# The beginning reordered: tokens first, quantiser in PSUM, key tiles ahead of the router, GpSimd in pieces of 512

## The reference

```python
x = x + matmul(fake_quant(layernorm(x)), fake_quant(ctx))         # per batch
x = x + moe(layernorm(x))     # 16 experts, 4 groups, top 2 groups, top 2 experts, 1 shared expert
x = x + cross_attention(layernorm(x), ctx)   # 32 heads, 8 KV heads, rms norm of q and k
x = x + lora_experts(x)       # 64 experts of rank 8, top 16

def fake_quant(x, scale, zp):
    return (clip(round(x / scale + zp), 0, 255) - zp) * scale
```

## Time and profile before

| | us |
|---|---|
| median of 3 runs (lowest, highest) | 688.44 (688.21, 688.82) |
| the profiled execution's own time | 687.87 |
| its span, first to last instruction | 686.1 |
| PE, DVE, ACT, POOL busy | 630.3, 435.5, 346.1, 326.9 |
| mean granted TensorE clock | 0.970 |

### The profile page before, as it was taken

One profiled execution on the slowest core, in us unless ns is written; L12 is line 12 of the kernel. 1 busy time (PEld: TensorE's weight loads), 2 busy tenths in 40 slices (PEclk: granted clock), 3 DMA queues, 4 the chain that ended last, 5 costly groups with the idle time before them and its releaser, 6 DMA issues.

```text
span 686.1 us, 11191 instructions
## 1 busy us (share of the span) xinstructions
PE 630.3 (92%) x3004; PEld 281.0 (41%) x3004; DVE 435.5 (63%) x991; ACT 346.1 (50%) x754; POOL 326.9 (48%) x310
## 2 busy tenths in 40 slices
PE   5729989889999999999998599999999979999997
PEld 2314534334444444444443134444444424444453
DVE  5999887354334443855555899999999950000673
ACT  4514535333334333476676677777777743143132
POOL 4923134255445552177878444444444433458111
PEclk9958999899999999999999999999999999999999
DMA  8802035444453433158794999999999995315001
GB/s 330 361 0 76 10 77 93 102 125 138 147 141 123 131 99 123 62 124 218 163 215 92 222 175 188 174 181 182 185 182 182 182 185 158 120 65 183 1 1 62
DMA packets 200314, 95.65 MB, mean 139 GB/s; under 512 B 187962, under 2 KB 188090, under 8 KB 197341
## 3 DMA queue, kind: packets, MB, share of 16 engines
q1 hardware_dynamic: 197490, 90.49, 55.3%
q10 hardware_dynamic: 2795, 4.79, 2.4%
HBM read 48.03 MB, written 1.09 MB: 72 GB/s over the span
## 4 chain that ended last, share of the span: by engine, by line
PE 60%; DVE 18%; issue 8%; POOL 7%; SPq 3%; ACT 2%; DMA 1%; DVEq 0%; POOLq 0%; ACTq 0%
PE ps L276 20%; PE ps L277 19%; PE ps L278 19%; POOL wsp L1042 4%; POOL hlr L1042 3%; SPq L367 3%; DVE st L1165 1%; DVE nw L1177 1%; DVE nw L1176 1%; DVE f32r L1181 1%; DMA stage<-in_first_chunks 1%; DVE xT L1240 1%; PE ps L615 1%; DVE v_sb L1217 1%; DVE nw L1178 1%
## 5 line engine op out<-in xcount | busy, mean ns | idle before, releaser
L1042 POOL TENSOR_TENSOR wsp<-stage,wsp 128x512 f16<-128x512 f32 (+1 forms) x93 | 134.5, 1470 | 140.3 <-ACT wsp L775 72.5
L920 ACT ACTIVATE f32r<-f32r,mneg 128x512 f32<-128x512 f32 x128 | 91.4, 715 | 29.7 <-DVE mneg L1404 29.7
L1042 POOL TENSOR_TENSOR hlr<-f32r,hlr 128x512 f16<-128x512 f32 x52 | 60.8, 1179 | 90.1 <-ACT hlr L828 56.4
L1404 DVE CUSTOM_DVE_ANT_0 f32r<-ps,nmask 128x512 f32<-128x512 f32 x128 | 82.4, 679 | 1.9
L1122 POOL TENSOR_SCALAR stage<-f32r,rinv 128x512 f16<-128x512 f32 x64 | 44.2, 704 | 46.3 <-DVE rinv L1409 46.3
L1122 POOL TENSOR_SCALAR hlr<-f32r,rinv 128x512 f16<-128x512 f32 x64 | 43.6, 695 | 47.0 <-DVE rinv L1409 45.4
L1323 DVE TENSOR_REDUCE ss<-f32r 128x4 f32<-128x512 f32 x48 | 32.9, 685 | 44.0 <-ACT f32r L816 43.9
L276 PE MATMUL ps<-k_sb,q_sb 128*128 (+1 forms) x128 | 48.8, 381 | 11.7 <-DVE mneg L1404 9.1
L276 PE MATMUL ps<-q_sb 128*128 128x512 f16 x128 | 50.1, 391 | 10.2 <-POOL q_sb L1042 7.4
L1373 DVE SCALAR_TENSOR_TENSOR f32r<-ps,par,f32r 128x512 f32<-128x512 f32 x18 | 13.5, 750 | 72.2 <-PE ps L278 71.6
L276 PE MATMUL ps<-xT,wsp 128*128 128x512 f16 x144 | 55.9, 388 | 2.6 <-DVE stage L1365 2.6
(11 more groups left out here) (231 smaller groups left out, 1350.4 us busy)
## 6 DMA issues: line engine op xcount, KB each, us to landing
stage<-in_moe SPq DMA_DIRECT2D x18, 512.0 KB, 3.7
stage<-in_wq SPq DMA_DIRECT2D x8, 1024.0 KB, 5.2
stage<-in_wo SPq DMA_DIRECT2D x8, 1024.0 KB, 5.1
stage<-in_moe SPq DMA_DIRECT2D x18, 256.0 KB, 3.3
hlr<-gates_dram ACTq DMA_DIRECT2D x18, 256.0 KB, 3.2
k_sb<-in_wkv SPq DMA_DIRECT2D x3, 1024.0 KB, 18.5
stage<-in_first_chunks SPq DMA_DIRECT2D x4, 512.0 KB, 5.4
q_sb<-in_ctx_nat SPq DMA_DIRECT2D x1, 2048.0 KB, 14.8
```

Source lines behind the costliest of these rows:

```text
L920: act.activation(f32r[:, j % 4, :], f32r[:, j % 4, :], ACT.Exp, bias=mneg[:, j % 4:j % 4 + 1], scale=-1.0, accum_out=psum_col[:, j % 4:j % ...
L1042: return pool.tensor_tensor(dst_lo, src, dst_hi, ALU.subtract)
L1404: dve.tensor_tensor_reduce(f32r[:, j % 4, :], ps[j % 4][:, :], nmask[:, qt, :], 0.125, BIG, ALU.add, ALU.min, mneg[:, j % 4:j % 4 + 1]).th ...
```

## The change

The parameters and the tokens are loaded ahead of the first chunks. The `lo` parts of the context's first chunks are made by POOL instead of DVE, ahead of the weights' in the same loop. The first layer norm's 128x4 values lie in bank 3 (`scratch`), apart from the running inverse root, and the quantiser's passes work in banks 0 to 3 instead of `f32r`; PE therefore waits for the quantised tokens (`s_xq`) between its batches 0 and 1 of the first value rows. POOL's 2048-wide operations are issued as four of 512. The value `lo` parts of head group 1 are made by PE and ACT: a matmul with `negone` (minus the identity) subtracts the `hi` part in the bank, and ACT copies the rest out (`v_residuals`, `v_low`); before, DVE did it. The second layer norm is transposed into banks 4 to 7, and its transposes and the router's logits stand between the first key tiles (`beside_keys`: residuals before tile 1, transposes before tile 2, router before tile 3, each tile waiting for the bank's main product to be added, `s_xu`). The router's softmax and group choice move on DVE to before the sums of key tile 3, and Exp on ACT to behind tile 2. Where code is only moved into a function, the lines are cut:

```diff
--- before.py
+++ after.py
@@ -267,6 +270,10 @@
+        def ln_bank(n, t):
+            return ps[4 + t] if n == 0 else ps[t]
         def words(ap):
@@ -287,10 +294,10 @@
+            sp.dma_start(par[:, 0:PAR_SC + 4], params).then_inc(s_par, 16)
+            sp.dma_start(x_sb[:, :, :], x_rows.rearrange("(t p) d -> p t d", p=P)).then_inc(s_x, 16)
             for c in range(KC):
                 sp.dma_start(stage[:, :, c * GW:(c + 1) * GW], first_chunks[c]).then_inc(s_first[c], 16)
-            sp.dma_start(par[:, 0:PAR_SC + 4], params).then_inc(s_par, 16)
-            sp.dma_start(x_sb[:, :, :], x_rows.rearrange("(t p) d -> p t d", p=P)).then_inc(s_x, 16)
             sp.dma_start(kv_land[:, 0, :], ctx_t).then_inc(s_ctx, 16)
@@ -420,24 +427,31 @@
+            def v_residuals(b):
+                for n in range(SC * b, SC * b + SC):
+                    pe.wait_ge(s_vh, NST + n + 1)
+                    pe.matmul(v_bank(1, n)[:, :], negone[:, :], v_sb[:, n, 0, GW:2 * GW],
+                              start=False, stop=True, skip_group_check=True).then_inc(s_vr, 1)
             def v_rows(hg, b):
-            def rms_phase(r0, iters, tiles, project, after_first=None):
+            def rms_phase(r0, iters, tiles, project, beside=None):
                         r = r0 + tiles * i + j
+                        if first and beside:
+                            beside(j)
                         if not first or j >= 4:
                 body(0, True)
-                if after_first:
-                    after_first()
                 with pe.Fori(1, iters) as i:
@@ -465,6 +479,8 @@
             for b in range(BATCH):
+                if b == 1:
+                    pe.wait_ge(s_xq, NT)
                 for c in range(KC):
@@ -537,22 +553,34 @@
             v_rows(1, 0)
-            ln_transposes(0)
...
+            def router():
+                pe.wait_ge(s_rws, 1)
+                for t in range(NT):
+                    ln_transposed(0, t)
+                    for c in range(KC):
+                        last = three_products(
+                            pe, ps[4][:, t * E_ROUTED:(t + 1) * E_ROUTED],
+                            [xT[:, t, l, c * P:(c + 1) * P] for l in range(2)],
+                            [rws[:, l, c * E_ROUTED:(c + 1) * E_ROUTED] for l in range(2)], c == 0, c == KC - 1)
+                last.then_inc(s_rt, 1)
+            def beside_keys(j):
+                if j < 4:
+                    pe.wait_ge(s_xu, j + 1)
+                if j == 1:
+                    v_residuals(0)
+                if j == 2:
+                    for t in range(NT):
+                        pe.wait_ge(s_vfree, NST + t + 1)
+                        ln_transpose(0, t)
+                if j == 3:
+                    router()
             pe.wait_ge(s_wlo, KC + 3)
-            rms_phase(0, 2, 8, k_project, lambda: pe.wait_ge(s_vfree, NST + 4))
+            rms_phase(0, 2, 8, k_project, beside_keys)
             first_expert()
@@ -581,6 +609,7 @@
             ln_transposes(1)
+            v_residuals(1)
@@ -761,7 +790,12 @@
                     act.wait_ge(s_lnT, NT * n + t + 1)
-                    act.copy(words(xT[:, t, :, :]), ps[t][:, :].rearrange("p (l w) -> p l w", l=2)).then_inc(s_lnTc[1], 1)
+                    act.copy(words(xT[:, t, :, :]), ln_bank(n, t)[:, :].rearrange("p (l w) -> p l w", l=2)).then_inc(s_lnTc[1], 1)
+            def v_low(tiles):
+                for n in tiles:
+                    act.wait_ge(s_vr, n + 1)
+                    act.copy(v_sb[:, n, 1, GW:2 * GW], v_bank(1, n)[:, :]).then_inc(s_vfree, 1)
@@ -799,15 +833,17 @@
             act.copy(b3[0], b3s[0:E_ROUTED + 1, :]).then_inc(s_b3h, 1)
+            v_hi(1, (0, 1, 2, 3))
             ln_hi(0)
-            v_hi(1, (0,))
+            v_low((0, 1, 2, 3))
             ln_copies(0)
-            v_hi(1, (1, 2, 3))
-            act.wait_ge(s_lg, 2)
-            act.activation(sml[:, 4:8, :], sml[:, 0:4, :], ACT.Exp).then_inc(s_rex, 1)
-            def rms_phase(r0, iters, tiles, scale, bias, s_T, landed, quarter=None):
+            def router_exponentials():
+                act.wait_ge(s_lg, 2)
+                act.activation(sml[:, 4:8, :], sml[:, 0:4, :], ACT.Exp).then_inc(s_rex, 1)
+            def rms_phase(r0, iters, tiles, scale, bias, s_T, landed, quarter=None, beside=None):
@@ -838,6 +874,8 @@
                                 quarter(i, j // 4, c)
+                        if first and j == 2 and beside:
+                            beside()
@@ -904,8 +942,9 @@
             ln_hi(1)
+            v_hi(1, (4, 5, 6, 7))
             ln_copies(1)
-            v_hi(1, (4, 5, 6, 7))
+            v_low((4, 5, 6, 7))
@@ -1044,6 +1083,7 @@
                 at = slice(c * GW, (c + 1) * GW)
+                low(ctxs[:, c, 1, 0:CTX], stage[:, 0, c * CTX:(c + 1) * CTX], ctxs[:, c, 0, 0:CTX]).then_inc(s_c0l, 1)
                 low(wkvs[:, 0, 1, at], stage[:, 1, at], wkvs[:, 0, 0, at]).then_inc(s_v0l, 1)
@@ -1053,11 +1093,16 @@
             for b in range(BATCH):
-                c32 = cnat[:, b * KC * D:(b + 1) * KC * D]
-                pool.tensor_scalar(c32, c32, scs[:, 5:6], scs[:, 3:4], ALU.mult, ALU.add).then_inc(s_c1, 1)
+                for c in range(KC):
+                    c32 = cnat[:, (b * KC + c) * D:(b * KC + c + 1) * D]
+                    last = pool.tensor_scalar(c32, c32, scs[:, 5:6], scs[:, 3:4], ALU.mult, ALU.add)
+                last.then_inc(s_c1, 1)
             for n, w in enumerate((3, 1, 2)):
                 pool.wait_ge(s_whi, KC + n + 1)
-                low(wkvs[:, w, 1, :], kv_land[:, w, :], wkvs[:, w, 0, :]).then_inc(s_wlo, 1)
+                for c in range(KC):
+                    at = slice(c * GW, (c + 1) * GW)
+                    last = low(wkvs[:, w, 1, at], kv_land[:, w, at], wkvs[:, w, 0, at])
+                last.then_inc(s_wlo, 1)
@@ -1168,6 +1213,16 @@
                 var, y, tmp = nw[:, 0, tiles], nw[:, 1, tiles], nw[:, 2, tiles]
+                if scratch is not None:
+                    var, bits, tmp = (scratch[:, NT * n:NT * (n + 1)] for n in range(3))
+                    link(dve.tensor_scalar(var, mv[:, tiles, 1], EPS, None, ALU.add))
+                    link(dve.tensor_scalar(bits.bitcast(I32), var.bitcast(I32), 1, None, ALU.arith_shift_right))
+                    link(dve.tensor_scalar(y.bitcast(I32), bits.bitcast(I32), -1.0, RSQRT_MAGIC, ALU.mult, ALU.add))
+                    for _ in range(3):
+                        link(dve.scalar_tensor_tensor(out=tmp, in0=var, scalar=-0.5, in1=y, op0=ALU.mult, op1=ALU.mult))
+                        link(dve.tensor_tensor(tmp, tmp, y, ALU.mult))
+                        link(dve.scalar_tensor_tensor(out=y, in0=tmp, scalar=1.5, in1=y, op0=ALU.add, op1=ALU.mult))
+                    return
                 link(dve.tensor_scalar(var, mv[:, tiles, 1], EPS, None, ALU.add))
@@ -1177,15 +1232,9 @@
-            def normalise(t):
-                return dve.tensor_scalar(f32r[:, t, :], x_sb[:, t, :], mv[:, t, 0:1], nw[:, 1, t:t + 1],
+            def normalise(t, out=None):
+                return dve.tensor_scalar(f32r[:, t, :] if out is None else out, x_sb[:, t, :], mv[:, t, 0:1], nw[:, 1, t:t + 1],
                                          ALU.subtract, ALU.mult)
-            for c in range(KC):
-                dve.wait_ge(s_c0h, c + 1)
-                dve.tensor_tensor(ctxs[:, c, 1, 0:CTX], stage[:, 0, c * CTX:(c + 1) * CTX], ctxs[:, c, 0, 0:CTX],
-                                  ALU.subtract).then_inc(s_c0l, 1)
@@ -1219,18 +1269,18 @@
             dve.wait_ge(s_x, 16)
-            layer_norm()
-            for t in range(NT):
-                last = normalise(t)
+            layer_norm(scratch=ps[3])
+            for t in range(NT):
+                last = normalise(t, ps[t][:, :])
             link(last)
             for t in range(NT):
-                last = dve.tensor_scalar(f32r[:, t, :], f32r[:, t, :], scs[:, 4:5], scs[:, 1:2], ALU.mult, ALU.add)
+                last = dve.tensor_scalar(ps[t][:, :], ps[t][:, :], scs[:, 4:5], scs[:, 1:2], ALU.mult, ALU.add)
             link(last)
             for t in range(NT):
-                last = dve.tensor_scalar(f32r[:, t, :], f32r[:, t, :], 0.0, QMAX, ALU.max, ALU.min)
+                last = dve.tensor_scalar(ps[t][:, :], ps[t][:, :], 0.0, QMAX, ALU.max, ALU.min)
             link(last)
             for t in range(NT):
-                dve.tensor_scalar(hlr[:, t, 0, :], f32r[:, t, :], ROUND, ROUND + MID, ALU.add, ALU.subtract).then_inc(s_xq, 1)
+                dve.tensor_scalar(hlr[:, t, 0, :], ps[t][:, :], ROUND, ROUND + MID, ALU.add, ALU.subtract).then_inc(s_xq, 1)
             v_lo(0, (0, 1))
@@ -1251,9 +1301,9 @@
                 dve.wait_ge(s_main, t + 1)
-                last = dve.scalar_tensor_tensor(out=x_sb[:, t, :], in0=ps[t][:, :], scalar=scs[:, 6:7],
-                                                in1=x_sb[:, t, :], op0=ALU.mult, op1=ALU.add)
-            link(last)
```

(43 more changed lines are left out.)

29 lines of the change are left out of this document (3 added, 26 removed).

## The result

| | us |
|---|---|
| changed kernel, median of 4 runs (lowest, highest) | 677.66 (676.49, 687.48) |
| kernel before, in the same session | 688.44 (688.21, 688.82) |
| ratio, 95% interval | 0.9837 (0.982 to 0.9854) |
| predicted | 678.4 (674.5 to 683.0), faster 0.92 |

The kernel became faster by 10.8 us, and the forecast stands 0.7 above the median. But one of the four executions took 687.48 us, as long as the kernel before, and that is the one that the profiler recorded (a fifth on record took 677.18). In this document the medians include such long executions, and the ratios leave them out. So there are two profiles to read: the usual one and the one with the accident. I begin with the usual one, of *again* (676.77 us, span 675.0).

The account below looks back on a forecast made before the run. The beginning was taken as bound by DVE, held by POOL, then by SP's queue of key transposes starting after the gates. 687.87 - 11.0 + 0.9 = 677.8, plus 0.57 to the median: 678.4 us, range 674.5 to 683.0.

Parts of the forecast that it names:

- Loads: Beginning: tokens land at 6.5 us, 6.4 earlier; chunks from 8.1, 3.4 later.
- Layer norm and quantiser in PSUM: First layer norm: twelve small steps undelayed by POOL, 3.0 us to 12.4; sixteen passes at 0.65 end at 22.9.
- the first rival: Small steps held in PSUM too, one POOL piece per step: 690.1 us, 4%; milder form 683, 7%.
- Context and main product: DVE's context operations alternate with POOL pieces, ending at 35.5; second value rows start at 41.9 instead of 58.4.
- What takes back part: POOL's late subtractions delay DVE's additions to 46.2 instead of 42.3, second small steps to 57.6 instead of 54.3.
- rival 3: PE falls cold, 2.6 us idle between tile 1 and transposes; tile 2 is 2 us later: 680.7 us, 20%.
- rival 2: DVE and POOL don't collide later, as POOL's pieces leave gaps of a few tens of ns: 675.8 us, 20%.
- Gates and queue: Router beside key tiles: gates end at 81.1, 11.0 us earlier, and with them the last 26 transposes and first expert.
- Second layer norm: Layer norm ahead of the queries: four more PE matmuls (0.9 us) on the path, +0.9.

Follow-up runs that it names:

- again: The changed kernel unedited, five more executions: median 676.51 us, ratio 0.9826 to the kernel before.
- sbuf: Changed kernel with the first layer norm and the quantiser back in SBUF and PE's wait between its batches dropped: 689.86 us, ratio 1.0015 to the kernel before.
- steps: Changed kernel with only the first layer norm's twelve 128x4 steps in PSUM, normalise and quantiser passes back in SBUF: 679.65 us, ratio 0.9889.
- load: Changed kernel with the four first chunks loaded ahead of parameters and tokens again: 683.4 us, ratio 0.9926 to the kernel before.
- hold: Changed kernel with POOL waiting for both of DVE's context batches before its twelve weight subtractions: 678.19 us, ratio 0.9856 to the kernel before.
- wide: Changed kernel with POOL's five wide operations 2048 columns wide again instead of pieces of 512: 682.51 us, ratio 0.9893 to the kernel before.
- lo_dve: Changed kernel with the value low parts of head group 1, batch 1, made by DVE again: 675.97 us, ratio 0.9815 to the kernel before.
- linked: Changed kernel with POOL waiting for the end of each of its twelve weight subtractions before issuing the next: 678.31 us, ratio 0.9858.

## Why the prediction was right, and where it was not

1. *Loads.* Tokens at 6.5: DVE's statistics began at 7.11. The first chunk was cast at 8.45 (8.1 predicted), PE started at 12.09 (11.6).
2. *Layer norm and quantiser in PSUM.* Steps to 12.4, as put, but by luck: they began 0.6 late and took 2.4 us instead of 3.0. The passes took 10.9 us at 0.62 to 0.74 each (0.65 put); the end 23.4 against 22.9. *sbuf* and *steps* show that the operands' place is the cause. Of the first rival nothing came.
3. *Context and main product.* POOL's pieces of the scaling took 0.75 us (*load*: eight in 6.00) where I had put 0.66, which PE's work hid. Second value rows from 41.69 (41.9 put), granted clock 1.00.
4. *What takes back part.* The additions took 6.34 us (6.6 put), the steps ended at 56.5 (57.6). Two of the small steps were held where I had put five; the idle time of PE ahead of the transposes was 1.65, not 2.6, and PE did not fall cold there, that is, to half its clock (rival 3). It did in *hold*: tile 2 ended 2.0 us later there, as put, but the gates only 1.1 and not 2.3. In *again* the clock fell later (0.50 from 83 to 86), after 5.27 us idle, in a key tile whose delay the queue of transposes hides. The gaps between POOL's pieces that I held in favour of rival 2 are not in the rows: four pieces of 1.15 us take 4.50 together.
5. *Gates and queue.* Gates 80.4 (81.1), first transpose 68.5 (70), first expert 122.9 (123).
6. *Second layer norm.* +0.63 instead of +0.9.

So the sum held term by term, within a microsecond each. What failed is a rule and not a term: "DVE's two operations per batch (1.2 each) alternate with POOL pieces", that is, a held DVE operation waits for at most the piece that runs. It held in six of the eight profiled executions in which this clamp meets the twelve pieces (2.17 us in each). In the recorded execution the same operation lost eleven boundaries in a row, and it took 14.39 us instead of 2.17; in *load* and *wide* the rule failed for the context's first batch. My range had no such case: its top was 683.0, and I wrote the first rival's 690.1 for the small steps, with a chance of 4%, and not for the context's quantiser, where it came about. The rows of before gave no warning: DVE's two steps of 3.95 us and more lie beside two wide operations of POOL, one each, so DVE did get in between them there. The error was to take what one execution shows for a bound.

What decides in one execution that DVE goes between the pieces and in the next that it doesn't is open. The offsets between the two starts are equal within 0.01 us (POOL 0.07 ahead of DVE in both held executions and in *again*), and DVE's idle time ahead, 0.23 in the held ones, is 0.22 in *again* but 0.23 in *lo_dve*, which was not held. That queued pieces are needed fits *wide*, where the clamp with one operation to meet waited for that one only, and fits *hold*; it is not proved by *linked*.

What each part is worth, undone alone and read at the first expert: all of PSUM 12.0 us, tokens first 6.9, key tiles ahead of the router 2.5; PE's residuals in the layer norm ahead of the queries cost 0.63. They don't add, since the whole gives 11.35: with the quantiser in SBUF nothing of the rest is left. The width of POOL's pieces is worth 7.1 in the profiled execution, where the clamp was held; between the medians it is 6.0, and against the faster three executions of *wide* 2 to 4.5. The context's `lo` parts on POOL and PE's residuals for batch 0 were not undone alone, so their worth is not known.

## What to carry to other kernels

Put small linked DVE steps where they have at most one SBUF input (a PSUM bank as scratch) when POOL works beside them; it was worth some 9 us here. Where a wide DVE operation with its operands in SBUF lies on the critical path beside a busy POOL, count in its worst price not POOL's running instruction but everything queued behind it without a wait, and order POOL's queue so that it waits there. Then look at what the later work of POOL meets instead. And run a kernel often enough to see its rare execution: a median of four hides one in ten.

## What I had not expected of the hardware

A DVE operation that started 0.07 us after POOL's first piece was held for all twelve, 14.39 and 14.40 us, and in another execution with the same offset for one, 2.17 us. Three wide operations in a row held it for 11.15 us, and the rest of one piece of 512 with two whole ones held it for 3.75 (*load*). In all four profiled cases in which this operation lost the first boundary it was held until POOL's row was empty. Being first in time did not help: DVE had asked before each of the eleven later pieces began.
